# The bias of the attention's v: one more matmul on TensorE, or an addition on VectorE

## What is computed

```
x = _ln(x, ln1_w, ln1_b)
qk = _silu(x @ Wqk.T + bqk)
v = _silu(x @ Wv.T + bv)
heads = qk[..., None, :] * gamma + beta          # four heads, then rotary positions
attn = relu(quad_q @ quad_k.T / G + bias) ** 2   # within groups of G = 64 tokens
lin_kv = lin_k.T @ v / n
gate = _silu(x @ Wg.T + bg)
out = gate * (attn @ v + lin_q @ lin_kv)
out = _ln(out @ Wo.T + bo, ln2_w, ln2_b)
x = _layernorm(x + out)                          # then the experts: shared + top 2 of 8
```

## Time and profile before

| | us |
|---|---|
| median of 3 runs (lowest, highest) | 954.27 (954.24, 957.13) |
| the profiled execution | 954.7 |
| its span | 952.9 |

### The profile page before, as it was taken

The page is one execution under the profiler, slowest core; times in us unless marked ns, Lnnn a source line. Parts: engine busy times, 40 slices in busy tenths (PEclk is TensorE's granted clock), DMA queues, the critical chain, the costliest instruction groups (busy, mean ns, idle before and its releaser), DMA issues.

```text
span 952.9 us, 17306 instructions
## 1 busy us (share of the span) xinstructions
PE 899.6 (94%) x5792; PEld 797.3 (84%) x5792; DVE 691.6 (73%) x1727; ACT 549.7 (58%) x1013; POOL 219.4 (23%) x156
## 2 busy tenths in 40 slices
PE   4999998998999989899999999999999999889994
PEld 3778787787788778799999999999999999879994
DVE  5789888889878589666665757576665998815746
ACT  6646655655646635466454555556455888734744
POOL 1000110001000000234353555535343555310000
PEclk9999999999999999999999999999999999989998
DMA  4142223223226422264565748565564877827302
GB/s 162 51 160 67 72 95 110 72 72 110 72 78 214 157 46 89 73 238 114 166 165 130 240 94 237 138 200 136 177 158 119 225 226 218 270 88 226 111 23 89
DMA packets 67255, 130.78 MB, mean 137 GB/s; under 512 B 13980, under 2 KB 52223, under 8 KB 59904
## 3 DMA queue, kind: packets, MB, share of 16 engines
q1 hardware_dynamic: 49872, 107.72, 33.6%
q0 software_dynamic: 13632, 18.69, 11.4%
q10 hardware_dynamic: 3696, 3.67, 1.1%
HBM read 98.18 MB, written 30.83 MB: 135 GB/s over the span
## 4 chain that ended last, share of the span: by engine, by line
PE 50%; DVE 8%; DMA 4%; issue 3%; ACT 1%; POOL 0%; DVEq 0%; SPq 0%; POOLq 0%; ACTq 0%
PE bank L1662 22%; PE bank L1737 21%; DMA k_wstage<-wall 3%; PE bank L1682 3%; PE bank L1688 3%; DVE s_hl L1583 2%; PE bank L1722 1%; DVE s_acc L1439 1%; DMA s_xb<-x_rows,s_token 1%; DVE s_until_map L1441 1%; DVE s_until_map L1440 0%; DVE k_wpj1l L1477 0%; POOL s_xb L1142 0%; DVE s_wfc0l L1477 0%; PE bank L1659 0%
## 5 line engine op out<-in xcount | busy, mean ns | idle before, releaser
L1268 ACT ACTIVATE s_h<-bank,k_bfc 128x512 f32<-128x512 f32 (+1 forms) x216 | 134.4, 622 | 204.9 <-PE bank L1737 183.4
L1583 DVE TENSOR_TENSOR s_hl<-s_h,s_hh 128x512 fp32r<-128x512 f32 (+1 forms) x216 | 131.8, 611 | 145.9 <-ACT s_hh L1272 144.8
L1152 POOL DMA_INDIRECT residual_sums<-s_y,s_dest x64 | 110.5, 1727 | 203.5 <-DVE s_y L1511 190.1
L1272 ACT ACTIVATE s_hh<-s_h 128x512 fp32r<-128x512 f32 (+1 forms) x216 | 122.9, 569 | 9.1
L1737 PE MATMUL bank<-k_uh,k_wfc1h 128*128 128x512 f32 (+1 forms) x384 | 121.8, 366 | 1.1 <-PEq L193 1.0
L1142 POOL DMA_INDIRECT s_xb<-x_rows,s_token x64 | 72.3, 1130 | 210.6 <-DVE s_dest L1453 174.2
L1662 PE MATMUL bank<-s_wpj0l,s_hh 128*128 128x256 f32 x384 | 108.1, 282 | 1.4 <-DVE s_hl L1583 1.4
L1662 PE MATMUL bank<-s_wpj0h,s_hh 128*128 128x256 f32 x384 | 107.9, 281 | 0.0
L1662 PE MATMUL bank<-s_wpj0h,s_hl 128*128 128x256 f32 x384 | 107.7, 280 | 0.0
L1662 PE MATMUL bank<-k_wpj1l,s_hh 128*128 128x256 f32 x352 | 101.2, 288 | 4.1 <-DVE s_hl L1583 4.0
L1662 PE MATMUL bank<-k_wpj1h,s_hl 128*128 128x256 f32 x352 | 99.8, 284 | 0.0
(11 more groups left out here) (338 smaller groups left out, 2204.6 us busy)
## 6 DMA issues: line engine op xcount, KB each, us to landing
k_wstage<-wall SPq DMA_DIRECT2D x42, 1024.0 KB, 6.3
s_acc<-wall SPq DMA_DIRECT2D x14, 1024.0 KB, 8.8
s_x_in<-x SPq DMA_DIRECT2D x8, 512.0 KB, 4.3
s_x_res<-x SPq DMA_DIRECT2D x8, 512.0 KB, 4.5
x_rows<-s_x SPq DMA_DIRECT2D x8, 512.0 KB, 3.5
residual_sums<-s_x SPq DMA_DIRECT2D x8, 512.0 KB, 4.2
x_parts<-s_x1h SPq DMA_DIRECT2D x8, 512.0 KB, 2.6
x_parts<-s_x1l SPq DMA_DIRECT2D x8, 512.0 KB, 3.3
```

The lines of the kernel that those rows point to most:

```text
L1152: pool.indirect_dma_start(RES, bass.IndirectOffsetOnAxis(dest[:, at:at + 1].bitcast(U32), 0), y[:, t, :], None, bounds_check=N + S - 1, co ...
L1268: nc.scalar.activation(h[j % 2][:, cols], b[:, cols], ACT.Gelu_apprx_tanh, bias=bfc[w][:, j:j + 1]).then_inc(h_ev, 1)
L1272: nc.scalar.activation(hh[j % RING][:, cols], h[j % 2][:, cols], ACT.Copy).then_inc(hh_rd, 1)
L1583: tt(hl[j % RING][:, cols], h[j % 2][:, cols], hh[j % RING][:, cols].bitcast(F32), ALU.subtract).then_inc(hl_rd, 1)
```

## The change

PE's matmul with the v bias goes, and so do the tile bv2, its memset and its preparation. The bias is loaded to all 128 partitions as `bv_all`. After heads, DVE waits for each v product, adds the bias, writes v in SBUF and counts `v_biased`. ACT's v silu waits for that and works in place in SBUF. The counts of prepared tiles go down by one.

```diff
-        bv2 = sb("bv2", [P, E], F32R)
+        bv_all = sb("bv_all", [P, E])
...
-        raw_bv, raw_bo = raw[0:BR, 3584:3584 + E], shared["bpj_raw"][1 - SHW]
+        raw_bo = shared["bpj_raw"][1 - SHW]
...
+        v_biased = sem("v_biased")
...
-            load(ld_c0, (raw_bv, a["rows"][:, 0, :]), (raw_bo[:, :], a["rows"][:, 1, 0:D]), (ones_raw[:, :], a["ones"]))
+            load(ld_c0, (bv_all[:, :], a["rows"][0:1, 0, :].to_broadcast([P, E])), (raw_bo[:, :], a["rows"][:, 1, 0:D]), (ones_raw[:, :], a["ones"]))
...
-            for tile in (bv2, bo2, *bpj):
+            for tile in (bo2, *bpj):
...
                     for t in range(TT):
-                        act.wait_ge(v_mm, 4 * b + t + 1)
-                        nc.scalar.activation(v[:, t, :], bank[t][:, :], ACT.Silu).then_inc(v_ev, 1)
+                        act.wait_ge(v_biased, 4 * b + t + 1)
+                        nc.scalar.activation(v[:, t, :], v[:, t, :], ACT.Silu).then_inc(v_ev, 1)
...
                     stt(heads[:, 0, :], qkr[:, 1, :], vec[:, GQ + 1:GQ + 2], heads[:, 0, :], ALU.mult, ALU.add).then_inc(heads_rd, 1)
+                if main:
+                    need(dve, u_mm, 4 * b)
+                    for t in range(TT):
+                        dve.wait_ge(v_mm, 4 * b + t + 1)
+                        tt(v[:, t, :], bank[t][:, :], bv_all[:, :], ALU.add).then_inc(v_biased, 1)
                 if o:
...
-            dve.wait_ge(zeroed, 4)
-            bias_rows(bv2[0:BR, :], raw_bv)
+            dve.wait_ge(zeroed, 3)
...
-                        mm(bank[t][:, :], ones2[:, :], bv2[:, :], start=True, stop=False)
                         for k in range(KD):
                             last_i = three(bank[t][:, :], xTh[:, k, cols], xTl[:, k, cols], wv[0][:, k, :], wv[1][:, k, :],
-                                           False, k == KD - 1)
+                                           k == 0, k == KD - 1)
```

More of the change, by code:

```diff
@@ L706, in fc @@
                     pe.wait_ge(split_s, 4)
-                    pe.wait_ge(tab_rd, 5)
+                    pe.wait_ge(tab_rd, 4)
                 need(pe, h_ev, j - 1)
@@ L750, in step @@
                         pe.wait_ge(wl_rd, 2)
-                        pe.wait_ge(tab_rd, 2)
+                        pe.wait_ge(tab_rd, 1)
                     for t in range(TT):
@@ L768, in step @@
                         pe.wait_ge(wl_rd, 4)
-                        pe.wait_ge(tab_rd, 3)
+                        pe.wait_ge(tab_rd, 2)
                     pe.wait_ge(ul_rd, 4 * b)
```

## The result

The changed kernel takes **996.16 us** (median of 4 runs, 995.96 to 998.31) against 954.6 us (954.24 to 957.13): a ratio of 1.043, interval 1.0408 to 1.0453, so 41.6 us slower. The profiled execution took 996.16 us with a span of 994.4 us.

A forecast was written before the change was run, and what follows sets the result against it. It took PE as fullest in the attention (34.58 of 35 us), DVE close behind (30.68); 28.8 us of block losses plus 8 us of slow clock, 36.8 on 954.3, gave 991 us, range 970 to 1,002.

The forecast's parts named there:

- PE's saving is lost in its own waits: Attention, block 5: the 0.93 us a block from removed bias matmuls all vanish in PE's wait for the logits copy.
- L585's start + 3.33 us: Third projection group: PE starts it 3.33 us after the old start of L585, standing 6.0 us in block 5.
- PE is the later side behind the stall: From kvl to the next block, PE, not DVE, comes later and carries the 5.1 us delay through.
- Single blocks: Attention losses: 5.1 us each in b = 0, 3, 5, 6; 2.0 in b = 1; 0.8 in b = 2; clock extra.
- b = 4: Block 4: 3.5 us lost, because its q ran at a slow clock and made PE late; stall about 4.5 us.
- b = 7: Block 7: 2.1 us lost, DVE being earlier without x statistics for a next block; no slow clock counted.
- a rival: Slow clock over whole blocks, or also paid by b = 7 and second stalls: 1,000 us and more, chance 0.09.
- The clock: PE at half clock behind stalls in b = 0, 3, 4, 5, 6: 1.6 us each, 8 us in all.
- The rival that the clock holds: The same PE stalls, but without a slow clock behind them: 983 us, chance 0.17.
- The experts: The second half, after the attention: starts later with PE's end but stays unchanged itself.
- Rival (2): PE bounds everywhere and the wait on DVE is covered, so 7.5 us are gained: 947 us, chance 0.04.
- Rival (3): Only DVE's added time counts, 8 x 2.4 = 19.2 us, PE's wait being made up later: 973 us, chance 0.10.

The follow-up runs named there:

- run 4: The changed kernel with a matmul on a tile of zeros ahead of each v product on PE: 995.4 us, 1.0416 of the kernel before.
- run 5: The kernel before with four DVE additions a block into a tile nobody reads, silus and bias matmuls as they were: 958.4 us, 1.004.
- run 3: The changed kernel with unused matmuls filling PE's stalls in blocks 0 and 3 to 7: 986.3 us, 1.0316 of the kernel before.
- run 6: The kernel before without the 32 bias matmuls, the v bias not added anywhere: 951.6 us, 0.9967.
- run 1: The changed kernel with only ACT's logits copy moved ahead of the four v silus: 966.3 us, 1.0112 of the kernel before.
- run 2: The changed kernel with DVE's additions moved ahead of the rotary product and heads, ACT's order kept: 965.2 us, 1.0103 of the kernel before.
- run 8: The changed kernel with ACT's logits copy and both normalizations ahead of the v silus, and block 0's additions ahead of heads: 962.0 us, 1.0064.

## Why the prediction was right, and where it was not

I forecast 991 us and slower with 0.94; it is 996.2 us, within the range. The steps, one by one:

- **PE's saving is lost in its own waits.** Right: run 4 brings the matmuls back for 1.5 us of attention and no visible change of the whole.
- **L585's start + 3.33 us.** Right: 3.42 us in block 5 (L591 has that line's place, and the additions start where it started). Of the 0.09 us, 0.05 lie between the end of the copy (221.82 + 0.20) and PE's start at 222.07, a hand-over that the sum had put at nothing; the rest lies with ACT, whose silus take 630 ns and not 600. PE's stall was forecast at 6.0 us and is 5.97.
- **PE is the later side behind the stall.** Right: kvl waits 1.64 us in block 5.
- **Single blocks.** b = 0 was forecast at 5.1 + 1.6 = 6.7 and is 6.95; b = 1 at 2.0 and is 2.02; b = 3, 5, 6 at 6.7 and are 6.4, 6.86, 6.75 (b = 6 by another mix: its own qk product ran slowly, so that its stall was 4.4 us and not 6). b = 2 was 0.8 and is 0.26: kvl comes 0.79 us later after the start of the qk product (26.56 us against 25.77), as forecast, but DVE's next wait, for the high part of x, shrinks from 1.16 to 0.64 us and takes 0.5 us back, which the sum had left out and run 5 shows too.
- **b = 4 was mis-sized:** 3.5 + 1.6 = 5.1 forecast, 6.5 measured, its stall 5.93 us and not about 4.5. I had taken over from the trace that its qk product runs at the slow clock and PE is late there. That was the aftermath of one wait of 3.0 us; the same wait in the changed kernel (3.04 us before 162.39) left the clock at full. A slow stretch behind a wait of that length is not a property of the block.
- **b = 7 was mis-sized:** 2.1 forecast, 3.6 measured. Its stall of 2.97 us slowed the clock, and I had counted the clock from 4.5 us on. That term was left to a rival.
- **The clock.** 1.6 us for each of five stalls, 8 us, were forecast; run 3 measures 9.2 us net over six, near 11 with the slow stretch of its own added (an estimate). So each was worth a little more than forecast, and there was one more. The row that I took the 1.6 us from is a window of 3.2 us; PE's wait in it is 3.02 us by the timeline, no longer than the third one, which left the clock at 1.00, so the rows had no length that tells the two apart. The rival that the clock holds is out. The Trainium skill's statement ("TensorE: Matmul & The Clock Gate", on the HAM oscillation) that a repeated wait can turn the array cold in each iteration held here for every stall of the blocks 0 and 3 to 7.
- **The experts** take 2.1 us more of the span in the profiled execution, unforecast. Their spread over executions covers that; I can't assign it.
- **Rival (2), PE bounds everywhere and the wait on DVE is covered,** is out: PE stands for ACT's copy in the changed kernel, and run 4 returns its matmuls almost free. Its premise holds for the kernel before, and so does the advice of the Trainium skill ("Perfetto Trace Analysis", Identifying the Most-Contended Engine) that points to PE: without matmul and addition the attention is 6.1 us shorter in run 6, near 7 with the slow start of block 0 set aside, and 7.5 was the most it could be.
- **Rival (3), DVE's time,** is out: 3.5 us of time alone in run 5, not 19.2, and the moved copy of run 1 gives 30 us with DVE's work unchanged.

The loss of 39.3 us in the attention thus splits in this way. Moving the logits copy gives back 29.0 us (364.38 - 335.35). Of these, 7.6 us are the slow clock in blocks 3 to 7, by run 3 (9.2 us less the 1.6 of block 0), and the other 21.4 us, by difference, are PE's standing itself. What remains in run 1, 10.3 us, is block 0 (6.9, the slow clock behind its stall included), block 1 (2.0, as much as DVE's time alone costs it in run 5) and 1.4 us in the others.

Of the 4.8 us between 36.8 forecast and 41.6 measured, 2.9 are b = 4 and b = 7, put 1.4 and 1.5 us too low, and 2.1 lie in the experts' half, where nothing can be assigned; b = 2, put 0.5 us too high, offsets a part.

## What to carry to other kernels

Before work moves from one engine to another, list what stands behind the waiting instruction on its engine and who waits for that: here a copy of 0.20 us, queued behind four silus, cost more than all the work that was moved. Read the start of the new wait from the timeline as the place in the new engine's own order, not as the end of the data's product. And where two engines are within a microsecond or two per iteration, as PE and DVE are here, there is little to win by an exchange between them: without the bias work anywhere the time falls by only 0.3%.

## What was not expected of the hardware

The granted clock behind short stalls is not a matter of their length alone. PE's waits of 3.0 us ahead of a qk product left it at 1.00 in two places (block 6 before, block 4 after) and were followed by a slow stretch in two others (block 4 before, block 6 after), as was the stall of 2.97 us in block 7. In run 2 those of 1.95 and 1.96 us were followed by one, those of 2.23 and 2.27 us were not. After stalls of 4.4 us and more inside the attention a slow stretch came each time. In those of 5.0 us and more the clock fell while PE stood, but so it did in the one of 3.12 us in run 8. What tells the short ones apart stays open.

ScalarE's silu from SBUF took 630 ns against 597 ns from PSUM for the same 128x512 (whose columns these are), in the changed kernel:

```profile
L587 DVE TENSOR_TENSOR s_v<-bank,s_bv_all 128x512 f32<-128x512 f32 x32 | 19.8, 682 | 0.0
...
L440 ACT ACTIVATE s_v<-s_v 128x512 f32<-128x512 f32 x32 | 19.4, 630 | 67.8 <-DVE s_v L587 67.8
```
